# Loading the attention's queries and keys in four parts behind the stores of chunks 2 to 5

## The chip, the cores and the metric

The kernel runs on one core of one Trainium2 chip. The metric is the device time of one execution in microseconds (us). TensorE (PE), VectorE (DVE), ScalarE (ACT), GpSimd (POOL) and SyncE (SP) run programs of their own and meet at semaphores. SP computes nothing: it issues DMAs, and each of its DMAs runs on the core's 16 DMA engines.

## The reference, cut to what matters

A two-layer network in float32 on x of 4 x 1024 x 256: attention, a feed-forward net with ternary weights, a state-space layer and a mixture of experts. Only the front of the first layer is touched:

```python
x = x + _L0_attn_ref(_layernorm(x, axis=-1), Wq, Wk, Wv, Wo, quadrant_weights)
# inside, with H = 16 heads of d = 16:
q = (x @ Wq).reshape(Bx, Tx, H, d).transpose(0, 2, 1, 3)   # k and v likewise
attn = softmax((q1 . k_eff1 + q2 . k_eff2) * h ** -0.5)    # k_eff: k's halves mixed by softmax(quadrant_weights)
out = einsum('bhqk,bhkd->bhqd', attn, v)
```

## The kernel before, in words

**The projection stage (lines 241 to 410).** The 4096 tokens are worked in NC = 8 chunks of 512. For a chunk DVE normalises (L93), PE transposes (L385) and multiplies the four 128-row blocks of queries and keys (L397, 24 matmuls), and then the values (L405). Each result is split in a high part, cast by ACT (L369), and a low part, subtracted by DVE (L341), both into the buffer `parts`, which has two halves: chunk c uses half c % 2. When the low parts of a chunk are there (semaphore `lo_ready`), SP stores the half to the DRAM tensor `qk_parts` (L257, 2 MB). ACT may write a half again only when the store of the chunk two before it has landed (semaphores `stored[h]`; they start at 16, and a store adds 16). PE keeps the values of chunk c behind the queries and keys of the same chunk.

**The loads.** The attention works in 16 units, one batch of 1024 tokens and four heads each. Its operands lie in `KQ[r]`. `load_qk(sp, u, r)` (L203 to L213) fetches a unit from `qk_parts` with 12 DMAs of 128 KB, each into 16 partitions: three groups of rows for the queries and three for the keys, in two halves of the partitions each. Each adds 16 to `kq_loaded[r]`. Units 0 and 1 are both of batch 0, so their rows come from chunks 0 and 1 alone. The projection stage loads these two; the later ones are loaded inside the attention.

**SP's order.** SP is a queue in program order. `chunks()` runs chunks 0 to 5 in a hardware loop and 6 and 7 behind it. Before the store of chunk 6, SP waits until all six stores before it have landed, issues both units' 24 loads, and only then the stores of chunks 6 and 7. At the end it waits for all stores (L261), and the block ends at a barrier of all engines.

**The attention (from L1830).** It begins with SP's loads of the feed-forward weights and PE's first pass (L1967) of units 0 and, in part, 1: scores whose row maxima DVE takes (L1845). PE's first matmul waits for `kq_loaded[0]`. The second pass (L2006) with ACT's exponentials (L1884) follows.

Of the kernel before, what the change touches and what calls it, by code (L numbers as in the profile page):

```python
# [5 lines left out]
F32 = mybir.dt.float32  # L6
# [7 lines left out]
ds = bass.ds  # L14

P = 128
BATCH, SEQ, D = 4, 1024, 256
# [4 lines left out]
CW = CT * P  # L22
NC = T // CW
# [4 lines left out]
H, HD = 16, 16  # L28
# [8 lines left out]
PAIR_Q = [0, 1, 0]  # L37
PAIR_K = [0, 0, 1]
KROWS = len(PAIR_Q) * HD
AROWS = KROWS + PARTS  # L40
HALF = P // 2
HR = HG // 2
# [55 lines left out]
def chunks(eng, body, first=False):  # L98

    if first:  # L100
        body(0, 0)
        body(1, 1)
    with eng.Fori(1 if first else 0, NC // 2 - 1) as i:
        body(2 * i, 0)
        body(2 * i + 1, 1)
    body(NC - 2, 0)
    body(NC - 1, 1)
# [26 lines left out]
def transformer_kernel(nc, ins, out):  # L134
# [12 lines left out]
    def sem(name):  # L147
        phase_sems.append(nc.alloc_semaphore(name))
        return phase_sems[-1]
# [9 lines left out]
    def sbuf(stack, name, shape, dt=F32):  # L159
        return stack.enter_context(nc.sbuf_tensor(name, shape, dt))  # L160

    with outer:
# [10 lines left out]
        with mid:  # L173
            ffw = FeedForwardWeights(sbuf, mid)
            with ExitStack() as st:
# [25 lines left out]
                KQ = [sbuf(st, f"KQ{r}", [P, 2, HR, SEQ], F32R) for r in range(2)]  # L201
                kq_loaded = [sem(f"kq_loaded{r}") for r in range(RING)]

                def load_qk(sp, u, r):

                    b, g = u // UPB, u % UPB
                    src = pqk.rearrange("s a k p t -> s a (k p) t").rearrange("s a (g h c) t -> s a g c h t", h=HG, c=HD)
                    for side, pairs in ((1, PAIR_Q), (0, PAIR_K)):
                        for j, part in enumerate(pairs):
                            for y in range(2):  # L210
                                row = HALF * y + HD * j
                                sp.dma_start(KQ[r][row:row + HD, side].bitcast(F32),
                                             src[1 - side, part, ds(g, 1), :, HR * y:HR * (y + 1), ds(SEQ * b, SEQ)].rearrange("g c h t -> (g c) h t")).then_inc(kq_loaded[r], 16)  # L213


                with ExitStack() as s1:
# [10 lines left out]
                    part = lambda h, m, a: parts[:, h, m // DK, a, m % DK]  # L227
# [4 lines left out]
                        sem(n) for n in ("quad_loaded", "quad_steps", "quad_max", "quad_exp", "k_mixed", "w_hi", "w_lo", "idz", "id_ready"))  # L232
                    xn_tr, xh_ready, xl_ready = sem("xn_tr"), sem("xh_ready"), sem("xl_ready")
                    qk_done, hi_ready, lo_ready = (sem(n) for n in ("qk_done", "hi_ready", "lo_ready"))
                    v_done, v_kept, parts_turn = sem("v_done"), sem("v_kept"), sem("parts_turn")
                    ones_set = sem("ones_set")
                    stored = [sem(f"parts_stored{h}") for h in range(2)]
                    with nc.Block() as block:  # L238
                        @block.sync
                        def _(sp):  # L240
                            for c in range(NC):
                                if c >= 2:
                                    sp.wait_ge(x_loaded[c % 2], 16 * (c // 2))
                                sp.dma_start(X[:, CT * c:CT * c + CT, :], x_tiles[:, CT * c:CT * c + CT, :]).then_inc(x_loaded[c % 2], 16)
                            for h in range(2):
                                sp.sem_inc(stored[h], 16)

                            def body(c, h):
                                if isinstance(c, int) and c == NC - 2:

                                    for h2 in range(2):
                                        sp.wait_ge(stored[h2], 16 * (NC // 2))
                                    for u in range(2):
                                        load_qk(sp, u, u)
                                sp.wait_ge(lo_ready, 2 * DK * (c + 2))
                                sp.sem_inc(parts_turn, 1)
                                sp.dma_start(pqk[:, :, :, :, ds(CW * c, CW)].rearrange("s a k p n -> p (s a k) n"),  # L257
                                             parts[:, h].rearrange("p s a k n -> p (s a k) n").bitcast(F32)).then_inc(stored[h], 16)
                            chunks(sp, body)
                            for h in range(2):  # L260
                                sp.wait_ge(stored[h], 16 * (NC // 2 + 1))  # L261

# [151 lines left out]
                with ExitStack() as s2:  # L414
                    attention(nc, sem, s2, sbuf, ps, KQ, kq_loaded, load_qk, V, slot, sums, packed, heads_moved, weighed, invert_sums, spread_inverses, weigh_heads, ffw)
# [1627 lines left out]
```

## Time and profile before

| | |
|---|---|
| median of 3 runs | 1903.34 us (1901.82 to 1905.7) |
| the profiled execution: its time, its span | 1897.99 us, 1895.5 us |
| busy: PE, DVE, ACT, POOL | 1633.4, 1215.1, 984.4, 431.2 us |
| SP waits for the last stores (L261) | 19.1 us |
| PE's first matmul of the attention idles before | 21.7 us |

Times below are microseconds from the start of the span. A slice of the page is 1895.5 / 40 = 47.4 us; its digit is a busy share in tenths. The projection stage and the pause behind it are the first two and a half slices, the attention runs from there to the eighteenth.

### The profile page before, as it was taken

The page shows a single profiled execution, that of the slowest core. Times are in us where ns is not written, and L with a number is a line of the kernel's source. Part 1 is how long each engine was busy: PE and PEld are TensorE (multiplying, and loading weights), DVE is VectorE, ACT ScalarE, POOL GpSimd, SP SyncE. Part 2 cuts the span into 40 slices and gives each one's busy share as a digit, 9 for nine tenths or more (in the row PEclk, how much of TensorE's full clock was granted, in tenths as well). Part 3 has the DMA queues.
Part 4 walks back from the last instruction along what each step waited for, and adds up shares of the span by engine and source line. Part 5 has one row for each costly group of instructions (what it writes and reads, how often), then busy time and mean ns, then how long its engine had stood idle before and what let it go on. Part 6 is the DMA issues. An engine that isn't in the chain of part 4 may idle for free. (4 is left out here: it accounts for less than half of the span.)

```text
span 1895.5 us, 33280 instructions
## 1 busy us (share of the span) xinstructions
PE 1633.4 (86%) x10504; PEld 1102.0 (58%) x10506; DVE 1215.1 (64%) x2121; ACT 984.4 (52%) x2005; POOL 431.2 (23%) x568
## 2 busy tenths in 40 slices
PE   5949999999999999988699958999888279999990
PEld 4824333333333333327588847989874169888880
DVE  6649999999999999602688686555465832222224
ACT  3412888888888888870444323434232135555442
POOL 3027000000000000000012145212122245565550
PEclk9955999999999999997799988999898589999995
DMA  5662233334443323000100021131306722222117
GB/s 194 208 176 35 41 40 53 42 52 62 56 67 41 53 41 53 19 9 17 12 1 0 1 57 46 46 89 45 90 1 200 244 87 66 66 64 66 62 65 271
DMA packets 117577, 134.55 MB, mean 71 GB/s; under 512 B 27028, under 2 KB 91560, under 8 KB 117352
## 3 DMA queue, kind: packets, MB, share of 16 engines
q1 hardware_dynamic: 104712, 107.60, 25.0%
q0 software_dynamic: 7584, 20.72, 3.4%
q10 hardware_dynamic: 5184, 4.98, 0.8%
q8 instruction: 56, 0.92, 0.2%
q14 instruction: 41, 0.34, 0.1%
HBM read 92.23 MB, written 36.04 MB: 68 GB/s over the span
## 5 line engine op out<-in xcount | busy, mean ns | idle before, releaser
L1845 DVE TENSOR_REDUCE mx<-ps 128x1 f32<-128x1024 f32 x512 | 602.1, 1218 | 56.7 <-PE ps L1967 56.2
L1884 ACT ACTIVATE PR<-ps 128x512 f32<-128x512 f32 x1024 | 533.1, 604 | 170.9 <-PE ps L2006 170.8
L1967 PE MATMUL ps<-KQ 48*128 48x512 f32 x1024 | 420.1, 488 | 28.5 <-PEq L238 21.7
L2006 PE MATMUL ps<-KQ 50*128 50x512 f32 x1024 | 375.2, 445 | 25.2 <-ACT PR L1884 10.7
L2006 PEld LDWEIGHTS ps<-KQ 50*128 50x128 f32 x1024 | 170.7, 185 | 329.9 <-ACT PR L1884 303.0
L1991 PE MATMUL ps<-PR,VO 128*32 128x512 f32 x2048 | 273.6, 606 | 2.1
L1967 PEld LDWEIGHTS ps<-KQ 48*128 48x128 f32 x1024 | 176.8, 196 | 80.0 <-DVE mx L1845 43.1
L1737 PEld LDWEIGHTS ps<-e_xinT,e_w 128*128 128x128 f32 x1264 | 154.8, 193 | 5.7 <-issue 1.7
L1727 PE MATMUL ps<-eW,e_hiddenT 128*128 x632 | 155.0, 388 | 3.4 <-issue 0.9
L1737 PE MATMUL ps<-e_xinT,e_w 128*128 128x128 f32 x1264 | 155.5, 277 | 1.1 <-ACT e_xinT L1669 1.1
L1697 DVE TENSOR_TENSOR e_y<-ps,b2b 128x256 f32<-128x256 f32 x79 | 33.6, 425 | 172.7 <-DMA expert_outputs<-e_y,e_y_index 163.6
L1904 POOL COPY VO<-V 128x512 f32<-128x512 f32 x16 | 9.8, 612 | 565.8 <-PE ps L1991 565.7
L1727 PEld LDWEIGHTS ps<-eW,e_hiddenT 128*128 128x128 f32 x632 | 113.7, 190 | 27.6 <-issue 14.5
L1173 PE MATMUL ps<-W 128*128 128x128 f32 (+7 forms) x512 | 112.9, 303 | 15.3 <-DVE W L987 13.7
L1174 PE MATMUL ps<-W 128*128 128x128 f32 (+7 forms) x576 | 115.3, 289 | 0.0
L731 PE MATMUL ps<-f_xT,wfT 128*128 128x512 f32 x384 | 96.1, 408 | 11.4 <-DVE f_xT L652 11.4
L1677 ACT COPY e_w<-eW 128x1024 f32 x79 | 82.6, 1045 | 27.2 <-issue 18.4
L1173 PEld LDWEIGHTS ps<-W 128*128 128x128 f32 x512 | 81.7, 195 | 23.3 <-DVE W L987 10.1
L1652 POOL DMA_INDIRECT expert_outputs<-e_y,e_y_index x79 | 79.2, 1002 | 64.7 <-POOL e_y_index L1649 63.0
L1643 POOL DMA_INDIRECT e_xin<-expert_inputs,e_index x79 | 77.9, 986 | 64.9 <-POOL e_index L1640 60.7
L1704 DVE TENSOR_SCALAR e_hiddenT<-ps,b1T 128x128 f32<-128x128 f32 x158 | 48.2, 347 | 68.4 <-issue 39.0
L731 PEld LDWEIGHTS ps<-f_xT,wfT 128*128 128x128 f32 x384 | 74.6, 197 | 28.5 <-DVE f_xT L652 9.5
(274 smaller groups left out, 2212.3 us busy)
## 6 DMA issues: line engine op xcount, KB each, us to landing
KQ<-qk_parts SPq DMA_DIRECT2D x192, 128.0 KB, 6.0
qk_parts<-parts SPq DMA_DIRECT2D x8, 2048.0 KB, 6.9
TB<-toeplitz_lines SPq DMA_DIRECT2D x32, 512.0 KB, 5.8
eW<-in_L_ffn_W SPq DMA_DIRECT2D x16, 512.0 KB, 6.9
eW<-in_L_ffn_W SPq DMA_DIRECT2D x8, 1024.0 KB, 12.0
e_got<-expert_outputs SPq DMA_DIRECT2D x16, 512.0 KB, 10.2
X<-in_L_attn_x SPq DMA_DIRECT2D x8, 512.0 KB, 4.8
V<-OT SPq DMA_DIRECT2D x64, 64.0 KB, 6.8
```

The source lines that it names most:

```text
L731: last = nc.tensor.matmul(ps[:, 2 + m % HB], w, x, start=(j == 0), stop=(j == len(todo) - 1))
L1173: nc.tensor.matmul(pair(0, h)[:, s % HS, 0:c + P], W2[:, s, P:2 * P], W1[:, s, P - c:2 * P], start=True, stop=True, skip_group_check=True)
L1174: last = nc.tensor.matmul(pair(1, h)[:, s % HS, 0:c + P], W1[:, s, P:2 * P], W2[:, s, P - c:2 * P], start=True, stop=True, skip_group_chec ...
L1652: nc.gpsimd.indirect_dma_start(y_rows, bass.IndirectOffsetOnAxis(ap=y_index[:, z:z + 1], axis=0), y[:, z], None).then_inc(stored[z], 16)
L1677: nc.scalar.copy(w1[:, z].rearrange("p k h -> p (k h)"), W1[:, ds(e, 1)].rearrange("p a k h -> p (a k h)")).then_inc(w1_kept, 1)
L1727: last = nc.tensor.matmul(ps[:, Y_BANK[z], 0:D], hT[:, z, j], W2[:, ds(e, 1), j, :].rearrange("p a d -> p (a d)"), start=(j == 0), stop=(j ...
L1737: last = nc.tensor.matmul(ps[:, bank, j % HK * P:(j % HK + 1) * P], w1[:, z, dk, j * P:(j + 1) * P], xT[:, z, dk], start=(dk == 0), stop=( ...
L1845: nc.vector.tensor_reduce(mx[:, u % RING, h * QT + q:h * QT + q + 1], ps[:, b:b + 2].rearrange("p a n -> p (a n)"), AX, ALU.max, negate=Tr ...
L1884: nc.scalar.activation(PR[:, kt % 2, h], ps[:, st_bank(u, s)], ACT.Exp).then_inc(exp_done, 1)
L1967: made = nc.tensor.matmul(ps[:, max_bank(u, t) + k], kq[half(h, KROWS), 1, h % HR, q * P:(q + 1) * P], kq[half(h, KROWS), 0, h % HR, k * B ...
L1991: last = nc.tensor.matmul(ps[2 * HD * h:2 * HD * (h + 1), OT_BANK], VO[:, u % 2, kt, h], PR[:, kt % 2, h], start=(kt == 0), stop=(kt == KT ...
L2006: nc.tensor.matmul(ps[:, st_bank(u, s)], kq[half(h, AROWS), 0, h % HR, kt * P:(kt + 1) * P], kq[half(h, AROWS), 1, h % HR, qc * BANK:(qc + ...
```

## The change

The 24 loads are no longer issued in one go ahead of the store of chunk 6. SP's chunk loop is written out; behind the store of chunk 2 it issues the first six loads of unit 0, behind that of chunk 3 the other six, behind chunks 4 and 5 the two halves of unit 1. Before each six it waits for `stored[0]` and `stored[1]` to reach 32, which chunks 0 and 1 alone bring them to. The loads and their order are the same. A semaphore that only counted SP's turns, `parts_turn`, is gone. No other engine's program changes.

```diff
-                def load_qk(sp, u, r):
+                def load_qk(sp, u, r, some=range(QK_LOADS)):
...
-                    for side, pairs in ((1, PAIR_Q), (0, PAIR_K)):
-                        for j, part in enumerate(pairs):
-                            for y in range(2):
-                                row = HALF * y + HD * j
...
+                    for n in some:
+                        side, j, y = 1 - n // (2 * len(PAIR_Q)), n // 2 % len(PAIR_Q), n % 2
+                        part = (PAIR_K, PAIR_Q)[side][j]
+                        row = HALF * y + HD * j
...
-                            def body(c, h):
-                                if isinstance(c, int) and c == NC - 2:
-
-                                    for h2 in range(2):
-                                        sp.wait_ge(stored[h2], 16 * (NC // 2))
-                                    for u in range(2):
-                                        load_qk(sp, u, u)
+                            FIRST_STORED = SEQ // CW
+                            for c in range(NC):
+                                h = c % 2
                                 sp.wait_ge(lo_ready, 2 * DK * (c + 2))
-                                sp.sem_inc(parts_turn, 1)
                                 sp.dma_start(pqk[:, :, :, :, ds(CW * c, CW)].rearrange("s a k p n -> p (s a k) n"),
                                              parts[:, h].rearrange("p s a k n -> p (s a k) n").bitcast(F32)).then_inc(stored[h], 16)
-                            chunks(sp, body)
+                                u, second = divmod(c - FIRST_STORED, 2)
+                                if 0 <= u < 2:
+                                    for h2 in range(2):
+                                        sp.wait_ge(stored[h2], 16 * 2)
+                                    load_qk(sp, u, u, range(second * QK_LOADS // 2, (second + 1) * QK_LOADS // 2))
```

## Rows read from the trace of the kernel before

**Rows 1.** The page, part 2: TensorE's clock and DMA share, 40 slices.
```profile
PEclk9955999999999999997799988999898589999995
DMA  5662233334443323000100021131306722222117
```

**Rows 2.** Waits of SP's queue, 0 to 190 us: total, times, longest.
```profile
SPq L256 <- DVE parts L341: 53.8, 6, 12.2
...
SPq L261 <- DMA qk_parts<-parts: 19.1, 1, 19.1
...
SPq L252 <- DMA qk_parts<-parts: 6.3, 1, 6.3
```

**Rows 3.** Timeline of SP's queue: start, length, line, what, count.
```profile
31.69 46.10 SPq L257 DMA_DIRECT2D qk_parts<-parts  x6
84.33 11.07 SPq L212 DMA_DIRECT2D KQ<-qk_parts  x24
95.53 3.31 SPq L257 DMA_DIRECT2D qk_parts<-parts  x2
...
77.41 0.37 SPq L257 DMA_DIRECT2D qk_parts<-parts  x1
```

**Rows 4.** Stores (L257), then loads from 84 to 120 us (L212): issue ns, landing.
```profile
L257 SPq DMA_DIRECT2D qk_parts<-parts x8: 372/384/2786, 31.7 to 96.0; - x8
...
DMA to landing us min/median/max: 6.8/6.9/21.9
...
L212 SPq DMA_DIRECT2D KQ<-qk_parts x24: 352/423/425, 84.3 to 95.0; - x24
...
DMA to landing us min/median/max: 3.2/8.3/12.8
```

**Rows 5.** Stretches: length, engines' busy time, then TensorE's clock, DMA share, GB/s.
```profile
50.00:52.00 2.00, 2.00 (x20) 2.00 (x19) 1.55 (x3) 0.42 (x1) 0.00 (x0) 1.00 0.49 186
...
56.50:57.00 0.50, 0.50 (x4) 0.40 (x3) 0.12 (x1) 0.35 (x1) 0.00 (x0) 1.00 0.03 8
60.00:60.50 0.50, 0.50 (x7) 0.50 (x6) 0.50 (x1) 0.00 (x0) 0.00 (x0) 1.00 0.78 291
...
83.50:84.00 0.50, 0.50 (x4) 0.42 (x3) 0.02 (x1) 0.42 (x1) 0.00 (x0) 1.00 0.58 213
...
85.00:85.50 0.50, 0.50 (x7) 0.50 (x6) 0.00 (x0) 0.50 (x1) 0.00 (x0) 1.00 0.50 90
86.00:105.00 19.00, 10.77 (x71) 9.59 (x69) 4.26 (x6) 5.22 (x7) 0.00 (x0) 0.91 1.06 149
...
106.50:107.00 0.50, 0.00 (x0) 0.00 (x0) 0.00 (x0) 0.00 (x0) 0.00 (x0) 0.50 0.91 283
107.00:116.00 9.00, 0.00 (x0) 0.00 (x0) 0.00 (x0) 0.00 (x0) 0.00 (x0) 0.50 1.05 409
116.50:117.00 0.50, 0.00 (x0) 0.00 (x0) 0.00 (x0) 0.00 (x0) 0.00 (x0) 0.50 0.48 184
...
220.00:232.00 12.00, 11.40 (x76) 4.30 (x74) 10.86 (x10) 10.18 (x21) 0.61 (x1) 1.00 1.07 137
```

**Rows 6.** Timelines of ACT and DVE, chunk 7: start, length, what, idle before.
```profile
90.00 0.59 ACT L369 CAST parts<-ps 128x512 fp32r<-128x512 f32 x1 [0.41 <-PE ps L397]
...
96.81 1.01 ACT L373 COPY V<-ps 128x1024 f32<-128x1024 f32 x1 [2.16 <-PE ps L405]
...
94.68 0.69 DVE L341 TENSOR_TENSOR parts<-ps,parts 128x512 fp32r<-128x512 f32 x1 [0.68 <-ACT parts L369]
```

**Rows 7.** Stretches behind the projection and in the attention, columns as in rows 5.
```profile
102.00:103.00 1.00, 0.00 (x0) 0.00 (x0) 0.00 (x0) 0.00 (x0) 0.00 (x0) 0.50 1.14 156
120.00:175.00 55.00, 48.84 (x84) 21.04 (x85) 51.39 (x47) 6.43 (x20) 41.24 (x37) 0.50 0.26 64
175.00:182.00 7.00, 7.00 (x25) 3.27 (x24) 6.39 (x6) 4.48 (x8) 4.48 (x2) 0.50 0.54 74
...
200.00:780.00 580.00, 558.06 (x3540) 220.42 (x3536) 529.53 (x491) 470.13 (x913) 22.86 (x20) 1.00 0.34 50
```

More of the change, by code:

```diff
@@ L202, in transformer_kernel @@
                 kq_loaded = [sem(f"kq_loaded{r}") for r in range(RING)]
-                def load_qk(sp, u, r):
+                QK_LOADS = 4 * len(PAIR_Q)
+                def load_qk(sp, u, r, some=range(QK_LOADS)):
                     b, g = u // UPB, u % UPB
                     src = pqk.rearrange("s a k p t -> s a (k p) t").rearrange("s a (g h c) t -> s a g c h t", h=HG, c=HD)
-                    for side, pairs in ((1, PAIR_Q), (0, PAIR_K)):
-                        for j, part in enumerate(pairs):
-                            for y in range(2):
-                                row = HALF * y + HD * j
-                                sp.dma_start(KQ[r][row:row + HD, side].bitcast(F32),
-                                             src[1 - side, part, ds(g, 1), :, HR * y:HR * (y + 1), ds(SEQ * b, SEQ)].rearrange("g c h t -> (g c) h t")).then_inc(kq_loaded[r], 16)
+                    for n in some:
+                        side, j, y = 1 - n // (2 * len(PAIR_Q)), n // 2 % len(PAIR_Q), n % 2
+                        part = (PAIR_K, PAIR_Q)[side][j]
+                        row = HALF * y + HD * j
+                        sp.dma_start(KQ[r][row:row + HD, side].bitcast(F32),
+                                     src[1 - side, part, ds(g, 1), :, HR * y:HR * (y + 1), ds(SEQ * b, SEQ)].rearrange("g c h t -> (g c) h t")).then_inc(kq_loaded[r], 16)
                 with ExitStack() as s1:
@@ L234, in transformer_kernel @@
                     qk_done, hi_ready, lo_ready = (sem(n) for n in ("qk_done", "hi_ready", "lo_ready"))
-                    v_done, v_kept, parts_turn = sem("v_done"), sem("v_kept"), sem("parts_turn")
+                    v_done, v_kept = sem("v_done"), sem("v_kept")
                     ones_set = sem("ones_set")
```

## The prediction, made before the changed kernel ran

> **What bounds the kernel now.** I read the page's slices first. The reader sees that in the third slice the granted clock is 5 and the DMA share is 6: the only place in the first half of the kernel where TensorE's clock is down while the DMA engines are loaded [rows 1]. Then the waits of SP's queue: SP waits 19.1 us at L261 for the last stores, once [rows 2]. That wait stands between projection and attention. The timelines say what it waits for. ACT's last copy of the values ends at 96.81 + 1.01 = 97.8 [rows 6], so the projection has computed everything by then, but the stores of chunks 6 and 7 are issued only at 95.53 and 96.0, behind 24 loads that start at 84.33 [rows 3, 4]. The store issued at 96.0 lands 21.9 us later, at 117.9 [rows 4], and the barrier opens then. So from 97.8 to 117.9 the DMA queue alone is the bound.
>
> The stretches show what the queue does [rows 5]. Loads run at 149 GB/s with a share of 1.06, stores at 409: with either, all 16 engines are full. The loads do the slow part (24 x 131 KB = 3.15 MB in 21.1 us) and end at about 106.4; the two stores need another 10.4, until 116.7 (116.5 plus 0.48 of half a microsecond), and 1.2 us later the landing is seen. Before the loads the queue has holes: each store is issued when its chunk is ready, every (77.41 - 31.69) / 5 = 9.14 us [rows 3], and works only 5.5 us of that.
>
> **The change, part by part.**
>
> The holes, as shares of their half microseconds give them [rows 5]: chunk 2's store works from 52.0 - 0.49 x 2 = 51.0 to 56.5, chunk 3's begins at 60.1: 3.6 us empty. The pattern repeats with the period behind chunks 3 and 4: 3.6 us each. Chunk 5's store ends at 83.8, the loads begin at 85.25: 1.45 us, the wait at L252 for that store to be seen landed [rows 2]. Together 3 x 3.6 + 1.45 = 12.3 us of an empty queue between 51.0 and the end.
>
> What the change moves: 24 loads at 21.1 / 24 = 0.88 us each, so six take 5.3 us. Behind chunk 2's store they fill the 3.6 us hole and run 1.7 us into the next period; so do those behind chunks 3 and 4, and those behind chunk 5 fill the rest. With the order of the queue, from 51.0: store 2 to 56.5, loads to 61.8, store 3 to 67.2, loads to 72.5, store 4 to 78.0, loads to 83.3, store 5 to 88.8, loads to 94.0, store 6 to 99.5, store 7 to 104.7. The queue is never empty, since store 6 is issued at about 86.5 (77.41 + 9.14) and store 7 at 95.5. The landing is seen at 105.8 instead of 117.9. Both ways give 12.1 to 12.3; I take **12.2 us saved**.
>
> Issue time: 24 DMAs at 0.42 us are the same ones [rows 4]; six take 2.6 us behind each store, and the next store is 9.14 us behind, so SP is back in time. The removed wait and the removed increments are on no path; the written-out loop only changes SP's own instructions. The two new waits are met when they are reached: store 1 lands 6.9 us after its issue [rows 4], and chunk 2's store is issued 9.14 us after chunk 1's. Behind them on SP stand the six loads and the next store, which would be late only if they lasted over 6 us. Cost: nothing, bounds 0 to 1 us.
>
> One store needed 2.79 us to issue, the one at 96.0 [rows 4], with a store and about a dozen loads not landed. If SP is held so again behind chunk 5 or 6, the queue it feeds is full meanwhile; cost nothing, or 1 us (a store's start lag, 51.0 - 50.09) if it is held until the queue is empty.
>
> What is late next: ACT writes a half of `parts` again when the store two chunks before has landed. Store 5 now ends at 88.8 and is seen at 89.3 to 90.0; ACT's first write of chunk 7 is at 90.00 [rows 6]. Store 4 is seen at 78.5 to 79.2, its writer comes at 80.9. So the margin is used up but hardly passed. If ACT were 1 us late, DVE's last low part (ends 95.4 [rows 6]) and store 7's issue would be 1 us late as well, and the queue is busy with store 6 until 99.5: that cover is 99.5 - 96.5 = 3 us. Nothing on the path.
>
> How long six loads take among stores and computation is what no row shows. Below: 149 GB/s, measured both while the engines computed and after [rows 5]. Above: 137 GB/s, the 12 loads of a unit in the attention with other DMAs among them [rows 5]: 5.7 us for six, four times 0.45 more: 1.8 us less saved. A gain beyond 12.2 comes if loads into SBUF and stores out of it overlap; the most that gives is store 7 alone as the end, 95.5 + 0.9 + 5.2 + 1.2 = 102.8, or 15.1 us saved. I stay at 12.2, since the change from loads to stores at 106.4 shows neither a hole nor a share above that of loads alone.
>
> The Trainium skill speaks against that rate. "SBUF — State Buffer", section "Door 1: The DMA port swizzle", says that a transfer into 16 partitions reaches 4 of 16 ports, about 109 GB/s. By it six loads would take 7.2 us, the stage would end at 113.5 and 4.4 us would be saved. The trace differs for these very loads, 149 GB/s, and I keep the measured value.
>
> Behind the barrier nothing changes but its time: attention's first pass waits for `kq_loaded[0]`, complete by 72.5, and everything else starts from the barrier. TensorE's clock: before, PE stops at about 96.8 and the clock is at half by 102 [rows 7]. Now PE would pause from 96.8 to 106.3, beyond that point, so the first pass starts at half clock again, and costs what it did.
>
> **Sum.** The profiled execution took 1897.99 us (span 1895.5 and 2.5 around it); less 12.2 it would take 1885.8. It lies 5.4 us under the median of the runs. From the median: 1903.34 - 12.2 = **1891.1 us**.
>
> **The rivals.**
>
> *Clock back sooner.* The pause shrinks from 21.6 to 9.5 us. If TensorE came back at full clock, DVE would no longer wait for it: in the first pass it is busy 51.39 of 55.00 us [rows 7], so up to 3.6 us go, and the two steps that take 7 us from 175 at half clock would take 2 x 2.54 (580 us x 4 / 913 exponentials), 1.9 us less. Saved 12.2 + 5.5 = 17.7: 1885.6. Against it: the clock fell about 5 us into the pause, and then stayed at half with PE busy 89% of 55 us.
>
> *Overlap.* Loads cost nothing beside stores: 15.1 saved, 1888.2. Against it: the rows of the switch at 106.4.
>
> *The queue drains at each switch.* The eight switches between store and loads each cost what the last store pays from its last byte to landing, 1.2 us at most: 9.6, so 2.6 saved, 1900.7. For it: chunk 2's store is seen landed 0.5 us after its last byte (50.09 + 6.9 against 56.5). Against it: no hole at 106.4.
>
> *Sixes are slower than 24 in a row.* Neighbouring loads go to different partitions and may help each other along, which a group of six has less of. Midway between 5.7 us and the 8.3 below, six take 7.0: the stage ends at 84.6 + 4 x 7.0 = 112.6, 5.3 saved, 1898.0. For it: 24 in a row are all that the projection's rows show. Against it: 137 GB/s for twelve among other DMAs. The skill's port rule above is this case with 7.2 us, 1898.9, and shares its chance.
>
> *The backlog wins, slower than before.* Place: the queue behind chunks 2 to 5 and ACT's wait for a free half of `parts`. The stage ends at 84.6 + 4L, L being the time of six loads (105.8 at 5.3). It reaches 117.9 at L = 8.3; from there on the change loses. Each further microsecond costs 4; at L = 9.5, 1908. ACT's stall alone (3L - 16.6 for chunk 7, 11.9 at 9.5) stays behind the queue. Against it: L would have to be 1.6 times what both states of the engines show.
>
> *The change does nothing*, as another engine holds the barrier: excluded by ACT's end at 97.8.
>
> **How the numbers follow.** The forecast has 0.74, clock 0.05, overlap 0.06, slower sixes 0.06, draining 0.05, backlog 0.04. The range: below, the clock rival, 1885.0; above, 137 GB/s (+1.8), held issues (+2) and the runs' own spread of 2 us give 1897, and 1898 takes in half of the slower sixes. About 0.2% (3.8 us) is what a measurement of this kernel can tell. Faster by more: 0.74 + 0.05 + 0.06 and half of the slower sixes, 0.88; within: the other half and draining, 0.08; slower: the backlog, 0.04.
>
> **What would show it.** Right: the stretches from 52 to 104 us with a DMA share near 1 throughout, alternating near 385 and 149 GB/s; SP's last wait (now L261) about 10 us instead of 19.1; attention's first matmul at 106.3 instead of 118.4 (0.5 us behind the landing); the idle time before it near 9.5. The clock at half from about 102 to about 171.5. Wrong: holes in the DMA row at switches (draining); an idle time of ACT before chunk 7's first cast of over 3 us with the queue's end past 110 (backlog); the first pass at a clock above half (clock); and a time above 1899.5 or below 1884.

## The result: 17.3 us saved, and the profile after

| | before | changed |
|---|---|---|
| median (runs) | 1902.13 us (6) | 1884.88 us (6) |
| lowest to highest | 1898.0 to 1905.7 | 1882.16 to 1886.59 |
| profiled execution, span | 1897.99, 1895.5 | 1884.29, 1882.4 |
| attention's first DMA | 118.39 | 102.68 |

The ratio is 0.9907 (95% interval 0.9894 to 0.9920). Forecast were 1891.1 us and 12.2 saved, with a range that ended at 1885.0: the direction and the place were right and the size was too small.

The page's slices (47.1 us each here) against [rows 1]: the DMA share of the second slice rises from 6 to 9 and that of the third falls from 6 to 2, while the clock is still down in the third and fourth.

```profile
PEclk9956999999999999998799989999898589999995
DMA  5922333344333323000100011132307622212117
```

SP's queue shows the moved loads. First its timeline in the changed kernel (start, length, line, what, count; L254 are the stores, L214 the loads), against [rows 3]:

```profile
31.44 18.77 SPq L254 DMA_DIRECT2D qk_parts<-parts  x3
50.32 5.79 SPq L214 DMA_DIRECT2D KQ<-qk_parts  x6
58.95 0.38 SPq L254 DMA_DIRECT2D qk_parts<-parts  x1
59.44 4.23 SPq L214 DMA_DIRECT2D KQ<-qk_parts  x6
68.06 0.38 SPq L254 DMA_DIRECT2D qk_parts<-parts  x1
68.54 4.89 SPq L214 DMA_DIRECT2D KQ<-qk_parts  x6
77.17 0.38 SPq L254 DMA_DIRECT2D qk_parts<-parts  x1
77.64 6.08 SPq L214 DMA_DIRECT2D KQ<-qk_parts  x6
86.28 9.48 SPq L254 DMA_DIRECT2D qk_parts<-parts  x2
102.68 0.37 SPq L463 DMA_DIRECT2D wf<-in_L_ffn_w_fc  x1
```

Every store is issued when its chunk is ready, 9.1 us apart. SP's waits, against [rows 2]: 6.5 us for the last stores where there were 19.1, and the 6.3 us wait ahead of chunk 6 has gone.

```profile
SPq L262 <- DMA qk_parts<-parts: 6.5, 1, 6.5
SPq L214 <- DMA qk_parts<-parts: 0.4, 1, 0.4
```

The queue itself, in stretches of the changed kernel (length, busy time of PE, PEld, DVE, ACT, POOL, then granted clock, DMA share, GB/s), against [rows 5]:

```profile
58.50:61.50 3.00, 3.00 (x27) 2.92 (x26) 2.39 (x5) 1.09 (x2) 0.00 (x0) 1.00 1.06 131
64.00:67.00 3.00, 3.00 (x17) 2.50 (x16) 1.96 (x4) 1.43 (x3) 1.27 (x2) 1.00 1.05 407
69.00:72.00 3.00, 3.00 (x21) 2.67 (x20) 3.00 (x8) 1.31 (x2) 0.00 (x0) 1.00 1.06 160
74.00:77.00 3.00, 3.00 (x21) 2.64 (x20) 1.64 (x3) 1.48 (x3) 0.66 (x1) 1.00 1.05 408
78.50:80.50 2.00, 2.00 (x14) 1.80 (x14) 1.77 (x5) 0.87 (x1) 0.00 (x0) 1.00 1.03 262
86.50:88.50 2.00, 2.00 (x19) 2.00 (x18) 1.23 (x1) 0.33 (x1) 0.00 (x0) 1.00 0.96 285
94.50:96.00 1.50, 1.50 (x15) 1.50 (x15) 0.69 (x1) 0.13 (x1) 0.00 (x0) 1.00 0.00 0
96.50:101.50 5.00, 0.25 (x3) 0.05 (x1) 0.00 (x0) 1.01 (x1) 0.00 (x0) 1.00 1.03 385
101.50:102.00 0.50, 0.00 (x0) 0.00 (x0) 0.00 (x0) 0.00 (x0) 0.00 (x0) 0.50 0.51 184
```

The holes are filled, as forecast. But look at the rates where the loads run, the rows with 131, 160, 262 and 285 GB/s: each group of loads is faster than the one before it, at an unchanged share near 1. By 94.5 the store of chunk 6 is done, which was forecast for 99.5, and the queue stands empty until chunk 7's store begins to move at 96.2. That store alone ends the stage, at 101.8 instead of 104.7.

The trace also holds the start and the duration of each packet that the DMAs are cut into. The 768 data packets of the 24 loads have 4 KB each; grouped by six loads (mean ns of a packet, and all their time over 16 engines, in us):

```
                        group 1  group 2  group 3  group 4   time over 16 engines
before, 24 in one go      405      464      453      438       21.1
changed                   440      376      228      204       15.0
```

The stores pay a little of it back: the packets of the stores of chunks 2 to 7 take 33.5 us over 16 engines before and 34.6 in the changed kernel. Loads and stores together take 5.1 us less, and by 5.0 us chunk 6's store ended ahead of the forecast.

### The profile page after: what moved, and what is told of

Its sections match the earlier page's. It is cut to its first block and busy times, and to the rows that moved or that the text cites. A ratio compares the mean times of both kernels' runs of the same rounds, so it can differ in the third digit from the quotient of the medians.

```text
span 1882.4 us, 33251 instructions
## 1 busy us (share of the span) xinstructions
PE 1635.3 (87%) x10505; PEld 1101.4 (59%) x10506; DVE 1214.3 (65%) x2121; ACT 984.3 (52%) x2005; POOL 431.7 (23%) x568
## 5 line engine op out<-in xcount | busy, mean ns | idle before, releaser
L1698 DVE TENSOR_TENSOR e_y<-ps,b2b 128x256 f32<-128x256 f32 x79 | 33.5, 425 | 172.9 <-DMA expert_outputs<-e_y,e_y_index 163.8
L1174 PE MATMUL ps<-W 128*128 128x128 f32 (+7 forms) x512 | 112.8, 303 | 15.6 <-DVE W L988 14.0
## 6 DMA issues: line engine op xcount, KB each, us to landing
eW<-in_L_ffn_W SPq DMA_DIRECT2D x8, 1024.0 KB, 12.2
```

The source lines that it names most:

```text
L1174: nc.tensor.matmul(pair(0, h)[:, s % HS, 0:c + P], W2[:, s, P:2 * P], W1[:, s, P - c:2 * P], start=True, stop=True, skip_group_check=True)
```

## The experiments

Twelve runs were made, ten of them of different kernels; two repeat the changed kernel and the halves version. "Saved" is against the median of the kernel before on the same chip. The time of a single execution carries the clock's spread, of which more below. The span does not begin at the same point of the work in every profile: the attention's first DMA of the changed kernel comes at 102.03, 102.68 and 103.47 in its three. TensorE's pause ahead of the attention is the same in all three, 5.98 to 5.99 us (21.67 before), and it is the better measure of where a stage ends that leaves the computation alone:

```profile
102.73 1.22 PE L1968 MATMUL ps<-KQ 48*128 48x512 f32 x4 [5.98 <-PEq L240]
```

**The changed kernel again.** No edit.

> The changed kernel once more, beside the kernel before on the same chip. Stage theory: the whole gain is the earlier end of the projection stage, 15.7 us (first load of the attention at 102.7 instead of 118.4), and what differs from that is when TensorE's clock comes back in the attention. Then the medians stand 13 to 18 us apart, and among runs of one kernel the time falls by about 1 us for each 0.001 of mean granted clock. Rival: part of the gain lies later in the kernel; then the profile shows the attention's second unit, counted from its first load, earlier than before at equal clock.

1884.91 us (5 runs) beside 1900.46 (9 runs), ratio 0.9919 (0.9905 to 0.9933): 15.6 us saved. Its load packets took 446, 389, 258 and 193 ns, so the falling pattern repeats. Times and mean clocks of the six first runs: 1886.59 at 0.925, 1885.48, 1884.29 and 1886.08 at 0.928, 1883.03 at 0.929, 1882.16 at 0.930. From the lowest clock to the highest that is 0.9 us for each 0.001, as expected. The rival gets no support: from the attention's first DMA to the first one of unit 0's results (`packed_sums`) it takes 109.0 us in this profile and 106.0 in that of before, so nothing later in the kernel comes sooner.

**Units exchanged.**

```diff
-                                    load_qk(sp, u, u, range(...))
+                                    load_qk(sp, 1 - u, 1 - u, range(...))
```

> The loads of unit 1 go behind chunks 2 and 3, those of unit 0 behind chunks 4 and 5; nothing else. Out-of-step theory: what a group of six costs depends on its place in the queue (after the queue has not been empty for a while, the 16 engines are at different DMAs and do not all write the same few partitions); then the groups in order of time again run at about 130, 150, 270 and 290 GB/s at their slowest microseconds. Rival, the data: unit 1's loads are cheap by where they lie; then the two fast groups are now the first two, behind chunks 2 and 3. The stage's end stays at 102.7 in both.

1884.48 us, the attention's first DMA at 102.42. Packets: 413, 302, 193, 378 ns. The first three fall with their place and unit 0's queries, 440 when first, take 193 when third: it is not the data alone. The fourth group speaks against a plain rule of place too: it ran at 152 GB/s where out-of-step theory had about 290. Stretches of the second, third and fourth group:

```profile
68.00:70.00 2.00, 2.00 (x19) 2.00 (x19) 1.64 (x3) 0.33 (x1) 0.00 (x0) 1.00 1.05 192
76.50:78.50 2.00, 2.00 (x20) 2.00 (x19) 1.39 (x2) 0.94 (x1) 0.00 (x0) 1.00 0.97 302
85.50:88.50 3.00, 3.00 (x26) 2.95 (x26) 1.70 (x2) 1.24 (x2) 0.00 (x0) 1.00 1.05 152
```

**Loads and stores kept apart.** Each store waits for the six loads before it.

```diff
                                 sp.wait_ge(lo_ready, 2 * DK * (c + 2))
+                                if c > FIRST_STORED:
+                                    part_done = min(c - FIRST_STORED, 4)
+                                    sp.wait_ge(kq_loaded[(part_done - 1) // 2], 16 * (QK_LOADS // 2) * (2 - part_done % 2))
```

> Each store from chunk 3 to chunk 6 waits also for the six loads before it to have landed, so loads and stores never share the queue. Overlap theory: six loads cost 5.5 to 6.5 us each time (load packets near 500 ns throughout), and a drain of about 1.3 us per switch comes on top: the stage ends at 113 to 118, so most of the gain is gone. Rival, no overlap needed (loads are simply fast when there are only six): groups behind chunks 4 and 5 still run near 270 GB/s, and the stage ends before 108.

The attention starts at 118.19, so the whole stage gain is gone. The packets take 440, 445, 440 and 402 ns, 20.7 us over 16 engines, somewhat less than the 500 expected. Two things took the gain: 5.7 us more of load packets than in the changed kernel, and four new stretches between the last load packet of a group and the first packet of the next store, 8.7 us together, in which the queue is empty. The stretches inside the four groups:

```profile
58.50:61.50 3.00, 3.00 (x27) 2.92 (x26) 2.39 (x5) 1.09 (x2) 0.00 (x0) 1.00 1.06 133
...
72.00:75.00 3.00, 3.00 (x15) 2.46 (x14) 2.05 (x8) 1.45 (x3) 1.26 (x2) 1.00 1.03 124
86.00:89.00 3.00, 2.44 (x22) 2.24 (x20) 2.65 (x5) 3.00 (x6) 0.00 (x0) 1.00 1.07 131
100.00:103.00 3.00, 0.00 (x0) 0.00 (x0) 1.87 (x4) 2.48 (x5) 0.00 (x0) 0.78 1.08 146
```

The same sixes that ran at 262 and 285 GB/s run at 131 and 146 once no store is queued behind them. Being only six does not make them fast. The one time, 1895.75, is 4.7 below the median before although the stage ends no sooner; it is 2.2 below the profiled execution of before (1897.99), which had its full clock back as soon in the attention, and a single time doesn't separate that from the spread.

**The loads spread over 128 partitions**, in the kernel before. The queries and keys are then misplaced.

```diff
-                                sp.dma_start(KQ[r][row:row + HD, side].bitcast(F32), src[...])
+                                sp.dma_start(KQ[r][:, side, y, ds(SEQ // 4 * j, SEQ // 4)].bitcast(F32),
+                                             pqk[1 - side, part, 0, HD * g:HD * (g + 1), 0:HR * SEQ].rearrange("c (m n) -> c m n", n=SEQ // 4))
```

> The kernel before, with its 24 loads in one go, but each load's 128 KB goes to all 128 partitions in runs of 1 KB instead of to 16 partitions in runs of 4 KB (scores are then made of misplaced values; GpSimd also fills a quarter of the buffers at the end of the stage). Few-partitions theory: the rate of the loads is set by the 16 partitions they write, so it rises from 149 to above 300 GB/s, the 24 loads take 8 to 12 us instead of 21, and the stage ends at 106 to 110 instead of 118.4. Rival, the loads are slow by reading DRAM or by their number: the rate stays near 150 or falls, and the stage ends at 118 or later.

```profile
86.00:101.00 15.00, 11.05 (x73) 9.87 (x71) 4.54 (x6) 5.38 (x7) 0.00 (x0) 0.94 0.66 194
```

The attention starts at 113.96, and the loads move 194 GB/s at a share of 0.66, or 294 for a full share. Both were expected better, above 300 GB/s and at 106 to 110; now the issue is the bound: SP needs 598 ns for each instead of 423, and each lands 2.7 us after it. The point stands: packets of 1 KB take 50 to 60 ns, four of them half of what one of 4 KB into 16 partitions took. The slow rate is neither the DRAM read nor the number of loads, but the shape of the transfer. Whether it is the 16 partitions or the 4 KB runs this kernel cannot tell, since both were changed together.

**The last store in halves.**

```diff
+                                if c == NC - 1:
+                                    for m in range(2):
+                                        sp.wait_ge(lo_ready, 2 * DK * (c + 1) + DK * (m + 1))
+                                        sp.dma_start(pqk[m:m + 1, ...], parts[:, h, m:m + 1]...).then_inc(stored[h], 16)
+                                    continue
```

> The changed kernel, but the last store goes in two halves, queries' parts when their two low parts are there, keys' parts when theirs are. Last-store theory: in the changed kernel the end of the stage is chunk 7's store alone (issued 95.4, seen landed 102.1), the queue being empty from 94.5 to 96.2; half of it now goes into that hole, and the stage ends 2.5 to 2.8 us sooner, at about 100. The median falls by 2 to 4 us. Rival, the queue's backlog still sets the end: no change within 0.5 us. If the clock does not fall in the shorter pause, another 3 to 5 us.

```profile
100.73 0.74 PE L1974 MATMUL ps<-KQ 48*128 48x512 f32 x4 [4.07 <-PEq L240]
```

The attention's first DMA comes at 100.69 and TensorE's pause is 4.07 us instead of 5.98, so the stage is 1.9 us shorter, less than the 2.5 to 2.8 expected. The median is 1881.26 (6 runs, 1877.43 to 1885.91), 19.6 saved, ratio 0.9906 (0.9890 to 0.9921); the changed kernel was not run on this chip. The clock fell at 101.3, just behind the start of the first pass.

**TensorE kept busy over the pause.**

```diff
                             chunks(pe, body)
+                            for j in range(24):
+                                nc.tensor.matmul(ps[:, j % 2], wsplit[0][:, 0, 0, 0:P], xT[0][:, 1, 0], start=True, stop=True)
```

> The changed kernel, and TensorE adds 24 matmuls of 128x128 by 128x512 behind its last chunk, 5 to 6 us of work into banks that nobody reads, so that its pause before the attention shrinks from 6 us to about 0.5. Clock theory: the clock fell at 101.8 because of the pause, and stays at full into the first pass; DVE then waits less (0.17 us per two reductions) and the first steps of the second pass run at full clock: 3 to 7 us faster. Rival: the first pass itself, with TensorE waiting for DVE, lets the clock fall a few us later; then the gain is under 1.5 us.

```profile
102.00:104.00 2.00, 0.74 (x4) 0.33 (x4) 1.24 (x1) 0.00 (x0) 1.75 (x1) 1.00 0.30 68
104.00:105.00 1.00, 0.00 (x0) 0.00 (x0) 1.00 (x2) 0.00 (x0) 0.95 (x2) 0.80 0.75 210
105.00:110.00 5.00, 4.15 (x8) 1.99 (x8) 4.63 (x5) 0.00 (x0) 2.13 (x3) 0.50 1.07 364
```

The clock now survives the pause and falls at 104.6, inside the first pass, while TensorE waits 2.6 us for DVE. The median is 1883.42 us (4 runs, ratio 0.9911, 0.9896 to 0.9927), 17.4 saved. The changed kernel was not run on this chip; on its three chips it saved 15.6 to 20.3, so no gain shows, as the rival had it. Filling the pause does not save the clock: the first pass loses it anyway.

**All loads behind the last store.**

```diff
-                                if 0 <= u < 2:
+                                if c == NC - 1:
...
-                                    load_qk(sp, u, u, range(...))
+                                    for u in range(2):
+                                        load_qk(sp, u, u)
```

> The changed kernel, but all 24 loads are issued behind the last store, so that no store waits behind a load and no hole is filled. The stage's barrier opens at 102.7 as in the changed kernel, but the attention's first matmul waits for unit 0's 12 loads, about 102 + 10.6 us + landing: 113 to 114. Hole theory: 10 to 11 us of the change's 15.7 are given back, the kernel is 4 to 6 us faster than before. Rival, the order alone (stores before loads) brings the gain: within 2 us of the changed kernel.

```profile
PE ps L1969 <- DMA KQ<-qk_parts: 18.9, 1, 18.9
```

TensorE's first matmul of the attention waits 18.9 us for the loads and starts at 116.65, 2.6 later than expected; the last 18 of the loads run at 517 ns a packet. 1895.77 us (10 runs), ratio 0.9975 (0.9964 to 0.9986): 5.0 saved. So stores ahead of loads are worth about 5 us, and putting the loads between the stores about 11 more. In those 11 two things are together, the filled holes and the cheaper loads: the load packets take 23.9 us over 16 engines here and 15.0 in the changed kernel.

**Two groups of twelve.**

```diff
-                                if 0 <= u < 2:
+                                if 0 <= u < 2 and second:
...
-                                    load_qk(sp, u, u, range(...))
+                                    load_qk(sp, u, u)
```

> The changed kernel with two groups of twelve, unit 0's behind chunk 3's store and unit 1's behind chunk 5's, instead of four of six. Packing rule without overlap: 12 loads take 10.6 us, so behind chunk 5 the queue is busy until about 104.5 and the stage ends at about 105.5. Out-of-step theory: the second twelve meet the next store and cost less; the stage still ends at 102.7 or at most 1 us later.

Both missed: the attention starts at 112.56. The 105.5 left out the first twelve, behind chunk 3, which delay stores 4 and 5. Counted from 61.7, where chunk 3's store begins, five stores of 5.3 and 22 us of loads end at 110.2; the bulk of the last store's data ends at 110.7. So the packing rule holds here with hardly any gain from overlap: the packets take 437, 512, 401 and 478 ns, although the queue is never empty from 61.7 on. Between the stores of chunks 2 and 3 the hole is back. The one time, 1894.56 us, is 6.3 below the median before. Stretches of the hole and of the two twelves:

```profile
59.00:61.00 2.00, 2.00 (x18) 1.91 (x17) 1.06 (x2) 1.29 (x2) 0.00 (x0) 1.00 0.00 0
70.00:78.00 8.00, 8.00 (x49) 6.97 (x48) 6.17 (x16) 3.56 (x6) 1.26 (x2) 1.00 1.06 131
91.00:99.00 8.00, 7.57 (x46) 6.51 (x44) 2.76 (x4) 3.12 (x6) 0.00 (x0) 1.00 1.05 140
```

**The last store in quarters, in halves, and the changed kernel, on one chip.** The quarters' edit is that of the halves with `for m in range(2 * DK)`.

> The changed kernel with chunk 7's store in four quarters, each issued when its low part is there. Last-store theory: in the halves version the queue's last work was half a store behind the last low part; with a quarter it is 1.3 us less, the stage ends near 99.4 (halves 100.7, changed kernel 102.7). The median comes 2 to 5 us under the changed kernel's of the same chip. Rival: seven DMAs' fixed times and the clock's late return eat it; then it is within 1 us of the halves version.

> The halves version again, on the chip of the quarters and of the changed kernel. Its stage ends at 100.7; the median lies 2 us (the stage alone) to 4 us under the changed kernel's.

> The changed kernel on this chip, to compare the two split versions with: about 16 us under the kernel before. Its four groups of loads should again fall in mean packet time with their place: 440, 380, 240, 200 ns.

| | median (4 runs each) | ratio, 95% interval | attention's first DMA |
|---|---|---|---|
| before (7 runs) | 1901.54 | | |
| changed | 1881.21 | 0.9899 (0.9882 to 0.9915) | 103.47 |
| halves | 1881.09 | 0.9897 (0.9880 to 0.9913) | 100.45 |
| quarters | 1882.93 | 0.9890 (0.9871 to 0.9909) | 102.06 |

The changed kernel's packets took 446, 391, 253 and 197 ns, as expected. TensorE's pause is 5.99 us in the changed kernel, 4.40 with halves and 5.85 with quarters: halves shorten the stage by 1.6 to 1.9 us, quarters by 0.1. Both expectations of the medians missed: on this chip halves are level with the changed kernel and quarters 1.7 us above it, and no version beats it beyond the spread. Why quarters give less than halves shows in their packets: the loads take 16.9 us over 16 engines instead of 15.3, and since in both versions the queue is never empty before the last store's end, that goes straight to the end of the stage. Why the loads were dearer there is open.

**Keys first.**

```diff
-range(second * QK_LOADS // 2, (second + 1) * QK_LOADS // 2)
+range((1 - second) * QK_LOADS // 2, (2 - second) * QK_LOADS // 2)
```

> The changed kernel, but each unit's six key loads go before its six query loads. With the units exchanged the fourth group was slow again (378 ns a packet against 193 for the third), which place in the queue alone does not explain. Place theory: 440, 380, 240, 200 ns in order of time here too. Data theory (unit 0's key rows are slow at any place): the first group is slow anyway, the second falls below 350, third and fourth are both below 260. The stage ends at 102.7 in both.

445, 413, 310, 225 ns, 16.7 us over 16 engines, the attention's first DMA at 102.47, 1884.10 us. It falls with the place, as one theory says, only more slowly; the data theory had the second group below 350 and the third below 260.

## Why the prediction was right in kind and short in size

**The bound and the holes: right.** The stage was the DMA queue's, the stores start on their chunks, the two new waits cost at most 0.4 us, and with all loads behind the last store 5.0 us are saved instead of 15.6 to 20.3. ACT's first cast of chunk 7 starts at 89.97 (90.00 before), so the margin that I called used up was not touched.

**The issue times: wrong in size, without a price.** I had six loads issued in 2.6 us, at 0.42 each. SP needed 5.8, 4.2, 4.9 and 6.1 us for its four groups, a median of 0.91 for each load. The last of a group was out at least 2.6 us before the next store, so the cost was nothing, as forecast, with a smaller margin.

**The step that failed: "six take 5.3 us".** I priced loads among stores by loads alone, 149 GB/s, and read the switch at 106.4 as a sign that nothing overlaps. That sign could not speak: the share is near 1 whatever the queue holds, and the packets show that stores and loads ran together for 1.9 us at that very switch, from 105.5, when the first packet of chunk 6's store starts, to 107.3, when the last load packet ends. All loads together took 15.0 us over 16 engines instead of the 21.1 I carried over, with 1.1 us more for the stores. Chunk 6's store was therefore done at 94.5 instead of 99.5, before chunk 7's could be issued, and the stage ended with chunk 7's store alone. That is the overlap rival, to which I gave 0.06: it had 102.8 for the landing; SP saw it at about 102.3. Its mechanism was right in kind, though "loads cost nothing beside stores" is not what happened: 15.0 us of 21.1 remained. The stage saved 118.39 - 102.68 = 15.7 us, not 12.2. The measured median, 1884.88, is nearest to the clock rival's 1885.6, and that is chance: what that rival needed, a first pass at full clock, did not come.

Why loads get cheaper: shown is that it needs stores close by in the queue (kept apart: 20.7 us; twelves: 22.0; sixes: 14.5 to 16.9 in nine profiles), and that 4 KB packets into 16 partitions are slow where 1 KB ones into 128 are not. A full queue alone is not enough, since the twelves had one. The packets' starts and durations say more than their means. Counted from them, the mean number of packets in flight while a load packet moves (itself included), group by group:

```
                           group 1   group 2   group 3   group 4
changed, ns of a packet      440       376       228       204
  load packets in flight     15.7      14.2      11.2      10.1
  store packets in flight     0.6       2.2       5.2       5.8
exchanged, ns of a packet    413       302       193       378
  load packets in flight     15.4      13.7      11.1      14.8
  store packets in flight     0.9       2.7       4.6       1.6
```

Over the thirteen profiles with 4 KB load packets, those with at least 16 load packets in flight took 463 ns, those with 8 to 12 took 269, those with fewer than 8 took 202. So the cheap groups are those whose packets mix with a store's, and the slow fourth group of the exchanged order is one that hardly mixed, so nothing about unit 0's keys is needed to explain it. The reading that fits is that the 16 engines, all on the same few loads, compete for the few partitions these write, and that engines which are at a store meanwhile leave the others faster. It stays a reading: the packets do not name their engine here, and the number in flight and the duration were only seen together. Why sixes mix more from group to group, why the exchanged order fell back, and why the twelves did not mix is open.

**The rate of the loads alone.** The Trainium skill, page "SBUF — State Buffer", section "Door 1: The DMA port swizzle", gives 109 GB/s for 16 partitions. By it 4.4 us would have been saved. The slowest stretches here were 124 to 131 GB/s, so for this stream of loads into changing rows the figure is too low, and the measured one decides. What I did not ask is what the limit means for the queue: if the destination limits a load, the engines may have time that other transfers can use.

**The clock: right that it falls, wrong on when it comes back.** TensorE's pause is 6.0 us, the clock is at half from 101.5, and the first pass runs at half, with DVE's two reductions every 2.53 us as before. But full clock came back at 176.6, not at the 171.5 forecast. Stretches of the changed kernel, and the corresponding one of the kernel before:

```profile
165.00:175.00 10.00, 10.00 (x42) 2.93 (x36) 5.75 (x5) 4.34 (x9) 0.00 (x0) 0.50 0.01 2
175.00:177.00 2.00, 2.00 (x12) 0.97 (x14) 1.01 (x1) 1.47 (x4) 0.00 (x0) 0.61 0.00 0
177.00:180.00 3.00, 2.94 (x24) 1.01 (x16) 2.77 (x4) 2.29 (x6) 0.00 (x0) 1.00 0.00 0
```

```profile
183.00:184.00 1.00, 1.00 (x8) 0.38 (x4) 0.45 (x1) 0.91 (x2) 0.00 (x0) 0.78 0.00 0
```

Before, full clock is back about 65 us after the attention's start, here about 74. From the attention's first DMA to the first one of unit 0's results (`packed_sums`) it takes 106.0 us before and 109.1 here: 3.1 us of the 15.7 are given back in this profile. The changed kernel's second profile has 109.0, its third, the same program, 105.9, the halves 106.0 and 105.9. So this is a property of an execution, not of the change, and it explains why the two profiled executions differ by only 13.7 us. The profile of before that I worked from had the cheap return and stood 5.4 us under the median; I noted the gap and did not ask what made it.

**What stays open.** The three comparisons of the changed kernel give 17.3, 15.6 and 20.3 us. Their mean, 17.7, is 2.0 above the stage's 15.7. The mean granted clocks point to an answer. The profile of before had 0.926, while of the 33 other executions of before whose clock is on record 31 had 0.922 to 0.925, most often 0.924; the changed kernel's profile had 0.928, the middle of its fifteen executions. At about 1 us for each 0.001, an estimate from the runs above, a usual execution of before is some 2 us dearer than the profiled one. Where in the kernel its clock was low was not seen, since before had one profile only.

## What to carry to other kernels

Price a transfer by what the whole queue then does, not by its rate alone: loads that write 16 partitions each keep all 16 engines "busy" at 131 GB/s, but mixed with stores the same loads cost as little as half of that (204 ns a packet against 438). When a move empties a bound queue, ask first which last item can't be moved, here the last chunk's store; it was the answer, and a row gave it. Before taking a profile's time as a base, look where it lies among the runs: this one was 5 us under the median, and the time of the clock's return alone can make 3 of them, against an effect of 17.

## What the hardware showed that was not expected

- Share near 1 does not mean that a queue can't take more: at shares of 0.96 to 1.07 the queue moved 124 to 408 GB/s, by what it held.
- Packets of the same loads took 174 to 517 ns in the mean of a group, by their company. The slowest, 512 to 517 ns, behind other loads with no store near, were slower than the 24 in one go before (405 to 464).
- Filling the pause did not keep the attention's first pass at full clock: with TensorE busy to 101.8 the clock still fell, at 104.6.
- The same program returned to full clock 65 or 74 us after the attention's start, at 3 us of difference in time.
